# Two 128-column products folded into one 256-column product in the wg0 unit of a fused graph-network and LSTM kernel

## The reference

```python
# x: 8 x 1024 x 128, adj: 1024 x 1024
h = relu(einsum('ts,bsh->bth', adj, x @ Wg0 + bg0))
h = relu(einsum('ts,bsh->bth', adj, h @ Wg1 + bg1))
for p in range(1, 5):                      # four LSTMs, windows of 1, 2, 3 and 4 nodes
    wins = h[:, :nw * p, :].reshape(B * nw, p, 128)
    last = lstm_last(Wih[p-1], Whh[p-1], bih[p-1], bhh[p-1], wins)
    h = h.at[:, arange(nw) * p + (p - 1), :].set(last)
x = layernorm(x + h)
```

## Time and profile before

| | before |
|---|---|
| median of 3 runs | 977.46 us (976.88 to 977.57) |
| the profiled execution's own time | 977.46 us |
| its span, first to last instruction | 975.7 us |
| TensorE busy | 960.5 us, 98% of the span |
| VectorE busy | 669.5 us, 69% |
| ScalarE busy | 442.5 us, 45% |
| granted TensorE clock, mean | 0.995 |

### The profile page before, as it was taken

One profiled execution on the slowest core, in us unless ns is written; L12 is line 12 of the kernel. 1 busy time (PEld: TensorE's weight loads), 2 busy tenths in 40 slices (PEclk: granted clock), 3 DMA queues, 4 the chain that ended last, 5 costly groups with the idle time before them and its releaser, 6 DMA issues.

```text
span 975.7 us, 13963 instructions
## 1 busy us (share of the span) xinstructions
PE 960.5 (98%) x5003; PEld 829.3 (85%) x5003; DVE 669.5 (69%) x1472; ACT 442.5 (45%) x809; POOL 36.0 (4%) x34
## 2 busy tenths in 40 slices
PE   9999999999999999999999999999999999999994
PEld 7888888888888888888988898898989889898894
DVE  7765677557575466754766656877676786877987
ACT  6354504434135342343433445446453555455765
POOL 0000200002000020000000001001010000100000
PEclk9999999999999999999999999999999999999998
DMA  8000010100110010205400000000000000000001
GB/s 308 1 1 1 1 44 35 53 1 2 42 55 31 0 43 1 87 1 204 174 1 1 1 1 1 1 1 23 1 1 23 0 22 0 21 1 22 1 2 65
DMA packets 11286, 30.99 MB, mean 32 GB/s; under 512 B 1120, under 2 KB 2400, under 8 KB 11232
## 3 DMA queue, kind: packets, MB, share of 16 engines
q1 hardware_dynamic: 11232, 30.30, 8.4%
HBM read 22.95 MB, written 7.34 MB: 31 GB/s over the span
## 4 chain that ended last, share of the span: by engine, by line
PE 95%; DVE 3%; ACT 1%; issue 1%; DVEq 0%; ACTq 0%
PE ps L875 25%; PE ps L1250 24%; PE ps L851 11%; PE ps L853 11%; PE ps L852 11%; PE ps L1303 3%; PE ps L1075 2%; PE ps L1323 2%; PE ps L893 2%; PE ps L1052 1%; PE ps L1171 1%; PE ps L1365 1%; DVE stats L1767 1%; PE ps L1397 1%; PE ps L1366 0%
## 5 line engine op out<-in xcount | busy, mean ns | idle before, releaser
L875 PE MATMUL ps<-adj,t 128*128 128x512 f32 x480 | 113.2, 390 | 0.0
L875 PEld LDWEIGHTS ps<-adj,t 128*128 128x128 f32 x480 | 89.3, 188 | 18.0
L1688 ACT ACTIVATE gates_x<-ps,lb 128x258 f32<-128x258 f32 (+1 forms) x156 | 66.5, 508 | 40.2 <-PE ps L1250 40.1
L851 PE MATMUL ps<-adj,node 128*128 128x512 f32 x216 | 84.5, 391 | 0.1
L875 PE MATMUL ps<-sx,t 128*128 128x512 f32 x360 | 84.4, 391 | 0.0
L853 PE MATMUL ps<-adj,node 128*128 128x512 f32 x216 | 84.3, 390 | 0.0
L852 PE MATMUL ps<-adj,node 128*128 128x512 f32 x216 | 84.2, 390 | 0.0
L1688 ACT ACTIVATE gates<-ps,lb 128x512 f32<-128x512 f32 (+2 forms) x117 | 66.7, 647 | 37.8 <-PE ps L1250 28.7
L1753 DVE SCALAR_TENSOR_TENSOR h<-ps,h 128x512 fp32r<-128x512 f32 x80 | 54.5, 688 | 37.2 <-ACT h L1480 37.2
L875 PEld LDWEIGHTS ps<-sx,t 128*128 128x128 f32 x360 | 67.1, 188 | 13.8
L1250 PE MATMUL ps<-hw,lw 128*128 128x258 f32 (+1 forms) x468 | 72.4, 303 | 0.0
(11 more groups left out here) (275 smaller groups left out, 1940.9 us busy)
## 6 DMA issues: line engine op xcount, KB each, us to landing
xb<-in_x SPq DMA_DIRECT2D x7, 1024.0 KB, 4.8
sx_raw<-in_adj_t SPq DMA_DIRECT2D x8, 512.0 KB, 8.6
adj_raw<-in_adj_t SPq DMA_DIRECT2D x8, 512.0 KB, 7.1
out<-xb SPq DMA_DIRECT2D x7, 512.0 KB, 2.6
xn<-xb SPq DMA_DIRECT2D x3, 1024.0 KB, 4.0
xb<-xn SPq DMA_DIRECT2D x6, 512.0 KB, 6.4
xb<-in_x SPq DMA_DIRECT2D x2, 512.0 KB, 5.1
lw_raw<-in_wih_t SPq DMA_DIRECT2D x1, 1024.0 KB, 11.0
```

Source lines behind the costliest of these rows:

```text
L851: pe.matmul(dst, stat(HI), mov(HI), start=start, stop=False)
L875: last = pe.matmul(dst, seven_block(e, B_BLOCK[v], a)[:, tile], A_BLOCK[v](b, t), start=start and t == 0 and (a, b) == (HI, HI), stop=t == ...
L1688: nc.scalar.activation(gates_in(u.stream)[:, g, at], ps[:, (AHEAD["gate"][slot] + gate) % GB, 0:u.n], ACT.Tanh if g == GG else ACT.Sigmoid ...
```

## The change

From slot 2 on (`side_by_side`), that is for six of the eight elements, the two terms that share z's high part become one product with a moving operand of 256 columns, Wg0 high and Wg0 low side by side. The 256 columns of a tile go side by side into PSUM; four tiles fill both banks 6 and 7. The third term (z low by Wg0 high) is accumulated onto the left 128 of each tile's 256. VectorE has to add the two parts: it adds low part and bias into `node_raw`, then the high part onto that. ScalarE and the low part's instruction read `node_raw` in place of PSUM. Since a `wg0` unit holds both banks, `bank_free` looks for any unit with a common bank, and after a `wg0` unit it waits for both additions (`bias_add`) and not for `b_lo`. In the lists SLOT and THIRD an `("ahead",)` moves from behind `("wg0", 1)` to between the two `wg0` units; in DRAIN the last tile of `adj_x` half 1 moves ahead of `("wg0", 0)`.

```diff
+        def side_by_side(slot):
+            return slot >= 2
+
+        def banks_of(slot, name, half):
+            return {GB, GB + 1} if name == "wg0" and side_by_side(slot) else {bank_of(slot, name, half)}
...
         SLOT = [step(Y, 1, 0), ("stats", 0, 8, 3), ("adj_x", 0, 0, 8), ("ahead",), step(X, 3, 0),
-                ("adj_x", 1, 0, 8), step(X, 3, 1), ("wg0", 0), ("wg0", 1), ("ahead",), step(X, 3, 2),
+                ("adj_x", 1, 0, 8), step(X, 3, 1), ("wg0", 0), ("ahead",), ("wg0", 1), step(X, 3, 2),
...
         DRAIN = [("ahead",), ("stats", 0, 8, 3), ("adj_x", 0, 0, 8), step(Y, 1, 0), ("adj_x", 1, 0, 7),
-                step(X, 3, 0), ("wg0", 0), ("adj_x", 1, 7, 8), step(X, 3, 1), step(Y, 1, 0, BANK, held=True),
+                step(X, 3, 0), ("adj_x", 1, 7, 8), ("wg0", 0), step(X, 3, 1), step(Y, 1, 0, BANK, held=True),
...
             "mm": lambda n: B_MM * (n < B),
-            "bias": lambda n: 2 * (n < B),
+            "bias": lambda n: (4 if side_by_side(n) else 2) * (n < B),
...
                 def bank_free(name, i):
                     mine = units_of(slot)
-                    held = [u for u in mine[:unit_at(slot, name, i)] if bank_of(slot, *u) == bank_of(slot, name, i)]
-                    if held:
+                    held = [u for u in mine[:unit_at(slot, name, i)] if banks_of(slot, *u) & banks_of(slot, name, i)]
+                    if held and held[-1][0] == "wg0" and side_by_side(slot):
+                        pe.wait_ge(bias_add, ahead("bias", slot, turn, 2 * (held[-1][1] + 1)))
+                    elif held:
                         lo_reached(b_lo_of(slot, *held[-1]))
...
                         v = item[1]
                         bank_free("wg0", v)
+                        if side_by_side(slot):
+                            for i in (HI, LO):
+                                if i == HI:
+                                    hi_reached(b_lo_of(slot, "adj_x", v))
+                                else:
+                                    lo_reached(b_lo_of(slot, "adj_x", v))
+                                for t in range(4):
+                                    nt = (4 * v + t) * P
+                                    dst = ps[:, GB + t // 2, t % 2 * 2 * F:t % 2 * 2 * F + (2 * F if i == HI else F)]
+                                    last = pe.matmul(dst, z[:, i, nt:nt + P],
+                                                     wgs[:, :, 0, :] if i == HI else wgs[:, HI, 0, :],
+                                                     start=(t % 2 == 0 and i == HI), stop=(i == LO),
+                                                     skip_group_check=True)
+                            last.then_inc(b_mm, 1)
+                            continue
...
-                        act.wait_ge(bias_add, ahead("bias", slot, turn, item[1] + 1))
-                        nc.scalar.activation(node[:, HI, cols], ps[:, bank_of(slot, *item[:2]), :], ACT.Relu).then_inc(b_hi, 1)
+                        wide = side_by_side(slot)
+                        act.wait_ge(bias_add, ahead("bias", slot, turn, (2 if wide else 1) * (item[1] + 1)))
+                        src = node_raw[:, cols] if wide else ps[:, bank_of(slot, *item[:2]), :]
+                        nc.scalar.activation(node[:, HI, cols], src, ACT.Relu).then_inc(b_hi, 1)
...
                         dve.wait_ge(b_mm, ahead("mm", slot, turn, unit_at(slot, "wg0", item[1]) + 1))
+                        if side_by_side(slot):
+                            def part_of_w(j):
+                                return ps[:, GB:GB + 2, :].rearrange("p b (t j c) -> p b t j c", t=2, j=2)[
+                                    :, :, :, j, :].rearrange("p b t c -> p (b t) c")
+                            raw = node_raw[:, cols].rearrange("p (t c) -> p t c", c=F)
+                            bias = bias0[item[1]][:].rearrange("p (t c) -> p t c", c=F)
+                            nc.vector.tensor_tensor(raw, part_of_w(LO), bias, ALU.add).then_inc(bias_add, 1)
+                            dve.wait_ge(bias_add, ahead("bias", slot, turn, 2 * item[1] + 1))
+                            nc.vector.tensor_tensor(raw, part_of_w(HI), raw, ALU.add).then_inc(bias_add, 1)
+                            hi_ready(b_lo_of(slot, "wg0", item[1]))
+                            lo_relu(node[:, LO, cols], node_raw[:, cols], node[:, HI, cols], b_lo)
+                            continue
```

## The result

| | before | after |
|---|---|---|
| median | 977.5 us (976.88 to 977.57) | 996.21 us (994.17 to 996.32, 4 runs) |
| ratio, 95% interval | | 1.0188 (1.017 to 1.0206) |
| span of the profiled execution | 975.7 us | 994.3 us |
| mean granted TensorE clock | 0.995 | 0.985 |

The change costs 18.7 us. The prediction said 9.6 us slower, 987.0, in a range of 983.5 to 990.5: the right sign, half the size, outside the range.

What follows compares the result with a forecast made beforehand. The prediction took TensorE, never idle in the slots, to bound the kernel. Five slots at 1.42 us (7.1) plus 2.46 in DRAIN made 9.6 us on 977.46, so 987.0 us, in a range of 983.5 to 990.5.

Steps and rivals of the forecast that it cites:

- What bounds the kernel: Slots: TensorE is busy 360.00 of 360.00 us, so a microsecond more or less in its queue moves the end.
- Products removed: wg0 units: a unit takes 0.93 us, a pair 1.86 against 2.63, saving 0.77; bounds nothing to 0.88 a pair.
- The new wait, and DRAIN: Unit 1, slots 2 to 6: idle 2.19, net 1.42 us (1.19 to 1.9); DRAIN unit 0: idle 3.26, net 2.46.
- The wait at adj_h: adj_h half 0 waits for unit 1's additions until S + 7.75; TensorE comes at S + 7.95, so it is covered.
- The sum: Whole kernel: 7.1 us for five slots plus 2.46 in DRAIN, 9.6 us slower, 987.0 us.
- rival 3: Behind the six new gaps TensorE's clock falls to 1.2 GHz, adding 12 us: 999; chance 0.05.
- rival 4: Slots: the waits are partly given back by something unseen, a gate chain late anyway: 977 to 983 us; chance 0.07.
- Rival 1: TensorE at unit 1: the waits are covered and the time falls by 4.6 us, to 972.8; chance 0.05.
- rival 2: wg0 products: the wide operand gives nothing, as two blocks of 128 that are not adjacent: 991.7 us; chance 0.05.

Runs made afterwards that it cites:

- run 1: Changed kernel with TensorE's waits filled by idle products, 9 ahead of wg0 unit 1 in slots 2 to 6 and 14 ahead of unit 0 in DRAIN: 986.97 us.
- run 8: Run 7 with unit 1's additions ahead of both low parts and adj_h half 0 starting with products that need high parts only: 974.46 us, ratio 0.9972.
- run 6: Run 1 with each wide product issued as two of 128 columns, and 7 idle products in place of 9: 990.42 us.
- run 7: Change in slots 2 to 6 alone, DRAIN as before, with VectorE doing unit 0's additions inside X31's cell: 977.14 us, ratio 0.9998.
- run 5: Kernel before, with X32's input products between the wg0 units and TensorE waiting ahead of unit 1 for unit 0's low part in slots 2 to 6: 1000.0 us.
- run 3: Change in slots 2 to 6 alone, DRAIN keeping its old list and narrow products: 989.86 us.
- run 2: Run 1 with 5 idle products in place of 9 in slots 2 to 6: 987.38 us.

## Why the prediction was wrong

*What bounds the kernel:* right. TensorE has no idle time in the slots, and delays and savings pass to the end nearly one for one (runs 1 and 8).

*Products removed:* right within its bounds. Unit 0's eight products take 699.11 - 698.25 = 0.86 us, 0.107 each, so the wide ones cost no more than the narrow ones, the lower bound that the forecast set beside its 0.93; unit 1 takes 0.97 (run 1). A unit saves 0.42 us against 0.39 (run 6).

*The new wait, and DRAIN:* right. The first addition stands at S + 3.55, an addition takes 0.68 to 0.69 us (the fifth more of the upper bound, for which no row stood, didn't come), and the start of X32's products is off by 0.02 us in slot 4, by 0.09 in slot 6. In DRAIN the stop for z's low part was read to 0.15 us: X30 starts 873.31 - 859.98 = 13.33 later than before, so unit 0 was due at 865.37 + 13.33 = 878.70, and starts at 878.55:

```profile
873.31 1.61 PE L1259 MATMUL ps<-hw,lw 128*128 128x344 f32 x9
878.55 1.97 PE L1333 MATMUL ps<-wgs,z 128*128 128x256 f32 x8 [2.95 <-DVE z L1776]
880.32 3.75 PE L1259 MATMUL ps<-hw,lw 128*128 128x344 f32 x12
883.87 2.59 PE L1259 MATMUL ps<-hstep_x,lw 128*128 128x344 f32 x12
```

*The wait at adj_h:* covered, as worked out. In slot 6, at the full clock, adj_h starts at 827.87 - 819.94, S + 7.93 (forecast S + 7.95).

*The sum:* this step failed. It took every product behind the waits at its full-clock price. In the rows above X31's input products take 883.87 - 880.32 = 3.55 us and not 1.95 (863.48 to 865.43 before). The sum needed a term for the clock, which the prediction put at nothing and left to rival 3; it measured 9.2 us by run 1, and without it the sum came out at half.

*The rivals:* rival 3 named this mechanism and priced it at 12 us for six falls of 2 us, 4 us at half rate each, a length that no row gave. Measured are five falls, of 3.4 us in the slots and 6.8 in DRAIN, and 9.2 us. The rival was given a chance of 0.05 on two rows: the one wait of 2.1 us in LAST, behind which the prediction saw no fall, and the stretch with 0.87 us of idle in ten at 1.00. The first was read wrongly. Behind that wait TensorE has four products and then nothing until the end, and its clock does fall, 1.8 us after they start (0.78 in the half microsecond from 966.5 is 0.22 us at half, so from 966.78). Three lines of the kernel before, one each of TensorE's timeline, of the busy times and of the groups by line:

```profile
964.97 0.66 PE L1397 MATMUL ps<-ident_f,hfull_last 128*128 128x128 f32 x4 [2.05 <-DVE hfull_last L2275]
966.50:967.00 0.50, 0.00 (x0) 0.00 (x0) 0.50 (x4) 0.50 (x3) 0.00 (x0) 0.78 0.00 0
L1375 PE MATMUL ps<-lw,wgs 128*128 128x512 f32 x13 | 3.4, 400 | 0.9 <-ACT gates_last L1688 0.9
```

A fall there had no work to slow, so the row says nothing of what a gap in the slots costs. The last line is the 13 idle products that the kernel before runs in LAST, `("busy", 6)` and `("busy", 7)`: the 1.00 of that stretch is that of a TensorE whose idle time is partly filled. And slot 6 of the changed kernel shows what a single row without a fall is worth: a gap like that of the other four slots, and no fall. The range had to reach to this rival, because the new gaps were, with that single one, the longest from 499 us on. (The range didn't reach rival 4 either, as the prediction says it does: 977 to 983 ends below 983.5.) Rival 1's turning point (additions 1.42 us earlier) is what runs 7 and 8 passed: in run 8 the first addition starts at 692.44 - 690.89, S + 1.55, 2.0 us earlier. Rivals 2 and 4 are out by runs 6 and 1.

*Open:* why slot 6 kept its clock, and why the clock stayed down twice as long in two slots of run 5 and in DRAIN. Slot 6 is not chance alone: the trace of run 3 has its falls in slots 2 to 5 too, and none in 6. No run told apart what, beside the gap's length, decides whether and when a fall comes.

## What to carry to other kernels

A wait put into a TensorE that was never idle has two prices: its length, and the clock behind it. Here five gaps of 2 us and one of 3 cost about as much again in clock as in delay (9.2 us beside 9.5), gaps of 0.9 us nothing; a gap between 0.9 and 2.0 us was not tried. Either fill them, keep them short, or count both. When an edit makes a unit wait for another engine, look where the releasing instruction stands in that engine's queue: here the same additions, moved into a pause 2 us earlier, turned 12.4 us slower into equal (runs 3 and 7), and more cover behind them made it 3 us faster.

## What was not expected of the hardware

The fall of TensorE's clock keeps no fixed distance from the gap. In the changed kernel, with the clock read in pieces of 0.1 us (times in us):

| | gap | products start again | clock falls | clock back at 1.00 | at the lower level |
|---|---|---|---|---|---|
| slot 2 | 2.06 | 581.25 | 581.3 | 584.7 | 3.4 |
| slot 3 | 2.00 | 642.38 | 642.7 | 646.1 | 3.4 |
| slot 4 | 2.00 | 703.26 | 704.1 | 707.6 | 3.4 |
| slot 5 | 2.00 | 764.12 | 765.6 | 769.0 | 3.4 |
| slot 6 | 2.00 | 824.95 | no fall | | |
| DRAIN | 2.95 | 878.55 | 878.2 | 885.1 | 6.8 |

In the slots it falls up to 1.5 us after the restart, in DRAIN 0.3 us before it, still in the gap. It comes back while TensorE is busy throughout. Over the traces of the changed kernel and of runs 3 and 5, 13 of 15 gaps of 2.0 to 2.3 us in the slots have a fall with them, and none of the five of 0.9 us in run 2. The restarts of the slots that are not shown above, and the microsecond in which DRAIN's clock falls:

```profile
581.25 1.97 PE L1333 MATMUL ps<-wgs,z 128*128 128x256 f32 x8 [2.06 <-DVE node_raw L2391]
642.38 1.72 PE L1333 MATMUL ps<-wgs,z 128*128 128x256 f32 x8 [2.00 <-DVE node_raw L2391]
764.12 1.14 PE L1333 MATMUL ps<-wgs,z 128*128 128x256 f32 x8 [2.00 <-DVE node_raw L2391]
824.95 1.13 PE L1333 MATMUL ps<-wgs,z 128*128 128x256 f32 x8 [2.00 <-DVE node_raw L2391]
878.00:879.00 1.00, 0.45 (x2) 0.45 (x3) 0.50 (x1) 0.00 (x0) 0.00 (x0) 0.61 0.00 0
```

Products of 128 columns with a weight load each run at 0.110 us, and a unit 0 in which half of them have 256 columns runs at 0.107. So the second 128 columns were nearly free for TensorE: 0.42 us of 1.39 saved in unit 1 (run 6).
